# First cross-attention of a decoder: keys and queries projected without padding, heads moved to their 32-row blocks by DMA

## The reference

```
def _L0_xattn_ref(query, key_value, Wq, bq, Wk, bk, Wv, bv, Wo, bo):
    scale = D ** (-0.5)                                   # D = 16, H = 16
    q = (query @ Wq + bq).reshape(B, Nq, H, D).transpose(0, 2, 1, 3)
    k = (key_value @ Wk + bk).reshape(B, Nkv, H, D).transpose(0, 2, 1, 3)
    v = (key_value @ Wv + bv).reshape(B, Nkv, H, D).transpose(0, 2, 1, 3)
    attn = jnp.einsum('bhqd,bhkd->bhqk', q, k) * scale
    attn = jax.nn.softmax(jnp.clip(attn, -CLAMP, CLAMP), axis=-1)
    x = jnp.einsum('bhqk,bhkd->bqhd', attn, v).reshape(B, Nq, Cq)
    return x @ Wo + bo
...
x = _layernorm(x + _L0_attn_ref(x, ...))
x = _layernorm(x + _L0_xattn_ref(x, ctx_768, ...))
x = _layernorm(x + _L0_ffn_ref(x, ...))
```

## Time and profile before

| | |
|---|---|
| median of 3 runs | 1327.05 us (1320.21 to 1327.78) |
| the profiled execution | 1310.7 us, its span 1309.0 us |
| PE busy | 1163.7 us, 89% of the span |
| DVE, ACT, POOL busy | 56%, 43%, 7% |
| PE's granted clock, mean | 0.952 of full |
| A0 and X0 | 0 to about 465 us of the span |
| X0's steady part | about 220 to 440 us |

### The profile page before, as it was taken

How to read it: one execution, slowest core, us unless ns; L and a number is a source line. 1 busy time by engine, 2 the same in 40 slices (tenths; PEclk the granted TensorE clock), 3 DMA queues, 4 the chain that set the end, 5 groups by cost and what they waited for, 6 DMA issues and landing times.

```text
span 1309.0 us, 20311 instructions
## 1 busy us (share of the span) xinstructions
PE 1163.7 (89%) x7602; PEld 737.1 (56%) x7602; DVE 734.4 (56%) x1083; ACT 560.2 (43%) x1078; POOL 86.6 (7%) x126
## 2 busy tenths in 40 slices
PE   4998988898998864897799999999999999998886
PEld 2454443232322233786477777767777777776545
DVE  3447567888889747344265645654445554654322
ACT  1444424555555632120266654555334553453230
POOL 0112301000000002000000000000000000000120
PEclk8899778999999977999899999999999999999989
DMA  6011002000000020000533222323533333210000
GB/s 178 11 50 26 1 1 57 1 1 1 1 1 1 1 81 1 1 1 1 139 74 74 66 66 46 80 57 89 116 92 82 81 82 81 47 36 1 1 17 16
DMA packets 46819, 57.44 MB, mean 44 GB/s; under 512 B 12539, under 2 KB 25350, under 8 KB 46726
## 3 DMA queue, kind: packets, MB, share of 16 engines
q1 hardware_dynamic: 42966, 52.48, 16.4%
q10 hardware_dynamic: 3760, 3.67, 0.9%
HBM read 15.23 MB, written 3.15 MB: 14 GB/s over the span
## 4 chain that ended last, share of the span: by engine, by line
PE 77%; DVE 10%; issue 6%; ACT 3%; POOL 1%; DMA 1%; SPq 1%; POOLq 0%; ACTq 0%; DVEq 0%
PE p_unit L1529 20%; PE p_ring L1529 11%; PE p_ring L1630 9%; PE p_out L1653 8%; PE p_ring L1549 8%; PE p_ring L1596 7%; PE p_out L1619 6%; PE p_ring L1574 2%; PE p_unit L1715 2%; PE p_unit L1673 1%; DVE probT_b L1342 1%; PE p_ring L1588 1%; DVE stats L1245 1%; ACT prob_a L1130 1%; POOL m_z L1059 1%
## 5 line engine op out<-in xcount | busy, mean ns | idle before, releaser
L1148 ACT ACTIVATE probT_b<-p_ring 128x512 f32<-128x512 f32 x144 | 84.5, 598 | 260.0 <-PE p_ring L1630 259.6
L1312 DVE TENSOR_REDUCE halves<-p_ring 128x2 f32<-128x1024 f32 x128 | 155.6, 1219 | 44.2 <-PE p_ring L1574 44.0
L1342 DVE COPY probT_b<-p_ring 128x512 f32<-128x512 f32 x112 | 77.4, 691 | 173.7 <-PE p_ring L1630 173.7
L1294 DVE TENSOR_REDUCE nmax<-p_ring 128x2 f32<-128x1024 f32 (+1 forms) x128 | 155.9, 1218 | 23.3 <-PE p_ring L1549 23.3
L1130 ACT ACTIVATE prob_a<-p_ring 128x1024 f32<-128x1024 f32 x128 | 130.5, 1023 | 89.5 <-PE p_ring L1596 89.2
L1116 ACT ACTIVATE prob_b<-p_ring,nmax 128x512 f32<-128x512 f32 (+1 forms) x192 | 158.7, 835 | 2.9 <-DVE nmax L1294 2.6
L1549 PE MATMUL p_ring<-stacks 128*128 128x512 f32 x512 | 150.8, 416 | 4.5 <-ACT prob_b L1116 4.5
L1630 PE MATMUL p_ring<-ident,prob_b 128*128 128x128 f32 x1024 | 134.6, 274 | 0.0
L1630 PEld LDWEIGHTS p_ring<-ident,prob_b 128*128 128x128 f32 x1024 | 115.8, 141 | 27.7 <-issue 25.8
L1596 PE MATMUL p_ring<-x_q,x_kq 32*128 32x512 f32 x512 | 117.8, 646 | 0.2
L1549 PEld LDWEIGHTS p_ring<-stacks 128*128 128x128 f32 x512 | 87.0, 190 | 17.1 <-ACT prob_b L1116 5.1
(11 more groups left out here) (199 smaller groups left out, 1610.4 us busy)
## 6 DMA issues: line engine op xcount, KB each, us to landing
stacks<-splitH_b SPq DMA_DIRECT2D x144, 128.0 KB, 2.3
stacks<-splitL_b SPq DMA_DIRECT2D x144, 128.0 KB, 2.4
a_st<-a_image SPq DMA_DIRECT2D x64, 32.0 KB, 1.8
ctx_raw<-in_ctx ACTq DMA_DIRECT2D x1, 1536.0 KB, 15.2
x<-in_x ACTq DMA_DIRECT2D x2, 512.0 KB, 5.5
k_words<-in_L_ffn_k SPq DMA_DIRECT2D x1, 1024.0 KB, 6.7
a_wq<-in_L_attn_Wq SPq DMA_DIRECT2D x1, 1024.0 KB, 6.0
a_wo<-in_L_attn_Wpost SPq DMA_DIRECT2D x1, 1024.0 KB, 8.6
```

The source lines that it names most:

```text
L1294: nc.vector.tensor_reduce(nmax[:, n % 4, 0:heads], src, AX.X, ALU.max, negate=True).then_inc(done["M"], 1)
L1312: nc.vector.tensor_reduce(to, src, AX.X, ALU.max, negate=True).then_inc(done["M1"], 1)
L1342: keep_turned(dve, key, lambda o, i: nc.vector.tensor_copy(o, i)).then_inc(done["VD"], 1)
```

## The change

Keys and queries of X0 are projected in slices of 128 true columns, eight heads at once, so one product serves two groups: 12 units in place of 24. ACT empties them into a new tile `x0_dense` (three parts of 512: two for keys, one for queries), which holds one pair of groups. A new kind of "DS" step on SP then moves each head's 16 rows to its 32-row block of `x0_kq`: 12 DMAs of 16 partitions a group, 96 in all, counted on one semaphore for each place (`x0_spread`). The padding and the row of ones, which the padded weights used to produce, are written once, by two memsets of `x0_kq` on DVE ahead of the stream. The query's factor moves from the weights into ACT's instruction, and the spread copies of the weights fall away.

POOL rounds a group's three parts only when its 12 DMAs have landed. ACT may overwrite `x0_dense` only when the DMAs of the pair's second group have landed (`heads_whole`); the ring place is waited for on SP and no longer on ACT. S1 of a group comes at least five steps after its DS step.

The context transposes (cT) now all stand ahead of the keys. The keys of groups 2 and 3 (pair 0, 1) are projected in A0 of batch 1, after the first query unit. The pairs (1, 0) and (1, 1) are projected at the ends of groups 0 and 2 of X0; the ends of groups 1, 3 and 4 have no projection any more. The S1, S2, PV and transposes of X0 keep their steps.

```diff
--- before.py
+++ after.py
...
@@ -164,7 +164,7 @@
...
-        return age("KF", "q", L, b, g) >= 2 and all(age("KF", "k", L, b, g, h) >= 2 for h in range(2))
+        return age("DS", L, b, g) >= 5
...
-            if u[0] in ("k", "q") and u[1] == "X0":
-                sched.add("KF", *u)
...
-    def x0_keys(b, g):
-        n = 4 * b + g - HELD
-        return [unit("k", "X0", b, g, h, after=used(8 + n) if n >= 0 else []) for h in range(2)]
-
-    def x0_queries(b, g):
-        n = 4 * b + g - HELD
-        return [unit("q", "X0", b, g, after=[turned_x("A0", b)] + (used(8 + n) if n >= 0 else []))]
+    def x0_heads(b, c):
+
+        G = 4 * b + 2 * c
+        out = [unit("k", "X0", b, c, s, after=[("DS", ("X0", (G - 1) // 4, (G - 1) % 4))] if G else []) for s in range(2)]
+        out.append(unit("q", "X0", b, c, after=[turned_x("A0", b)]))
+        for g in (2 * c, 2 * c + 1):
+            n = 4 * b + g - HELD
+            out.append(step("DS", "X0", b, g, after=[UA("q", "X0", b, c)] + (used(8 + n) if n >= 0 else [])))
+            out += [step("KF", b, g, part) for part in range(3)]
+        return out
...
-        [unit("cT", sg, c) for sg in range(2) for c in range(2)] + x0_keys(0, 0) + x0_keys(0, 1)
-        + [unit("cT", sg, c) for sg in range(2, 4) for c in range(2)] + x0_keys(0, 2)
-        + x0_keys(0, 3) + [u for g in range(4) for u in x0_keys(1, g)],
-        [q for b in range(B) for g in range(4) for q in x0_queries(b, g)],
+        [unit("cT", sg, c) for sg in range(4) for c in range(2)],
+        [it for b in range(B) for c in range(2) for it in x0_heads(b, c)],
...
-        x0_wq = sb("x0_wq", [128, 2, 512], into=first)
-        x0_wk1 = sb("x0_wk1", [128, 512], into=first)
+        x0_wq = sb("x0_wq", [128, 2, C], into=first)
+        x0_wk1 = sb("x0_wk1", [128, C], into=first)
+        x0_dense = sb("x0_dense", [128, 3, 512], into=first)
...
+
+            n = 4 * b + g
+            eng.wait_ge(x0_spread[n % HELD], 16 * 12 * (n // HELD + 1))
...
-            sp.dma_start(wq_in[:, :, :], rows("L0_xattn_Wq")).then_inc(x0_loaded, 16)
-            sp.dma_start(wk_in[:, 0, :], d["L0_xattn_Wk"][0:128, :]).then_inc(x0_loaded, 16)
-            sp.dma_start(wk_in[0:CC - 128, 1, :], d["L0_xattn_Wk"][128:CC, :]).then_inc(x0_loaded, 16)
-            sp.dma_start(wk_in[64:65, 1, :], d["L0_xattn_bk"].rearrange("(o n) -> o n", o=1)).then_inc(x0_loaded, 16)
+            sp.dma_start(x0_wq[:, :, :], rows("L0_xattn_Wq")).then_inc(x0_loaded, 16)
+            sp.dma_start(x0_wk0[:, :], d["L0_xattn_Wk"][0:128, :]).then_inc(x0_loaded, 16)
             sp.wait_ge(pads_cleared, 1)
+            sp.dma_start(x0_wk1[0:CC - 128, :], d["L0_xattn_Wk"][128:CC, :]).then_inc(x0_loaded, 16)
+            sp.dma_start(x0_wk1[64:65, :], d["L0_xattn_bk"].rearrange("(o n) -> o n", o=1)).then_inc(x0_loaded, 16)
             sp.dma_start(x0_wv0[:, 0:C], d["L0_xattn_Wv"][0:128, :]).then_inc(x0_loaded, 16)
             sp.dma_start(x0_wv1[0:CC - 128, 0:C], d["L0_xattn_Wv"][128:CC, :]).then_inc(x0_loaded, 16)
             sp.dma_start(x0_wv1[64:65, 0:C], d["L0_xattn_bv"].rearrange("(o n) -> o n", o=1)).then_inc(x0_loaded, 16)
-            bq = d["L0_xattn_bq"].rearrange("(g a p) -> a p g", a=4, p=16)
-            for a in range(4):
-                sp.dma_start(x0_bq[32 * a:32 * a + 16, :], bq[a], allow_slow_non_contiguous=True).then_inc(x0_loaded, 16)
+            sp.dma_start(x0_bq[:, :], d["L0_xattn_bq"].rearrange("(c p) -> p c", p=128),
+                         allow_slow_non_contiguous=True).then_inc(x0_loaded, 16)
...
+                if L == "X0":
+                    grp = 4 * b + p
+                    place, c = grp % HELD, p // 2
+                    sp.wait_ge(heads_cleared, 1)
+                    wait(sp, "UA", "k", "X0", b, c, 0)
+                    wait(sp, "UA", "k", "X0", b, c, 1)
+                    wait(sp, "UA", "q", "X0", b, c)
+                    if grp >= HELD:
+                        wait(sp, "S2", *prob_items(PAIRS[8 + grp - HELD])[-1])
+                    for part in range(3):
+                        for a in range(4):
+                            at = 64 * (p % 2) + 16 * a
+                            sp.dma_start(x0_kq[32 * a:32 * a + 16, place, part, :], x0_dense[at:at + 16, part, :])\
+                              .then_inc(x0_spread[place], 16)
+                    continue
...
-            pool.wait_ge(x0_scaled, 1)
...
-                    u = key
-                    _, L, b, g = u[:4]
-                    place, part = (4 * b + g) % HELD, u[4] if u[0] == "k" else 2
-                    wait(pool, "UA", *u)
+                    b, g, part = key
+                    place = (4 * b + g) % HELD
+                    heads_whole(pool, b, g)
...
-                        _, L, b, g = u[:4]
-                        place, part = (4 * b + g) % HELD, u[4] if u[0] == "k" else 2
-                        if 4 * b + g >= HELD:
-                            wait(act, "S2", *prob_items(PAIRS[8 + 4 * b + g - HELD])[-1])
+                        _, L, b, c = u[:4]
+                        if 4 * b + 2 * c:
+                            n = 4 * b + 2 * c - 1
+                            heads_whole(act, n // 4, n % 4)
                         if u[0] == "q":
-                            ins = nc.scalar.activation(x0_kq[:, place, part, :], p_unit[:, :], ACT.Identity,
-                                                       bias=x0_bq[:, g:g + 1])
+                            act.wait_ge(x0_scaled, 1)
+                            ins = nc.scalar.activation(x0_dense[:, 2, :], p_unit[:, :], ACT.Identity,
+                                                       bias=x0_bq[:, c:c + 1], scale=LAYERS["X0"]["D"] ** -0.5)
                         else:
-                            ins = nc.scalar.activation(x0_kq[:, place, part, :], p_unit[:, :], ACT.Copy)
+                            ins = nc.scalar.activation(x0_dense[:, u[4], :], p_unit[:, :], ACT.Copy)
...
-            for t in (x0_wv0, x0_wv1):
-                nc.vector.memset(t[:, :], 0.0)
-            nc.vector.memset(x0_bq[:, :], 0.0).then_inc(pads_cleared, 1)
+            nc.vector.memset(x0_wk1[:, :], 0.0)
+            nc.vector.memset(x0_wv1[:, :], 0.0).then_inc(pads_cleared, 1)
...
             nc.vector.memset(wide_max[:, :, :, :], 0.0)
-            nc.vector.memset(x0_wq[:, :, :], 0.0)
-            nc.vector.memset(x0_wk0[:, :], 0.0)
-            link(nc.vector.memset(x0_wk1[:, :], 0.0))
-            nc.vector.memset(x0_wk1[64:65, :].rearrange("p (h r) -> p h r", r=32)[:, :, 16], 1.0)
             nc.vector.memset(ctx_sum1[64:128, :], 512.0)
             nc.vector.memset(ctxT1[64:128, :], 1.0).then_inc(ctx_padded, 1)
+            nc.vector.memset(x0_kq[:, :, 0:2, :], 1.0)
+            nc.vector.memset(x0_kq[:, :, 2, :], 0.0).then_inc(heads_cleared, 1)
 
             for kind, key in sched.steps:
                 if kind == "XW":
-                    k = LAYERS["X0"]["D"] ** -0.5
                     dve.wait_ge(x0_loaded, 16 * X0_LOADS)
-                    for c in range(2):
-                        nc.vector.tensor_scalar(x0_wq[:, c, :].rearrange("p (h r) -> p h r", r=32)[:, :, 0:16],
-                                                wq_in[:, c, :].rearrange("p (h d) -> p h d", d=16), k, None, ALU.mult)
-                    nc.vector.tensor_copy(x0_wk0[:, :].rearrange("p (h r) -> p h r", r=32)[:, :, 0:16],
-                                          wk_in[:, 0, :].rearrange("p (h d) -> p h d", d=16))
-                    nc.vector.tensor_copy(x0_wk1[0:65, :].rearrange("p (h r) -> p h r", r=32)[:, :, 0:16],
-                                          wk_in[0:65, 1, :].rearrange("p (h d) -> p h d", d=16))
-                    nc.vector.tensor_scalar(x0_bq[:, :], x0_bq[:, :], k, None, ALU.mult).then_inc(x0_scaled, 1)
+                    nc.vector.tensor_scalar(x0_bq[:, :], x0_bq[:, :], LAYERS["X0"]["D"] ** -0.5, None, ALU.mult)\
+                      .then_inc(x0_scaled, 1)
...
-                        wait(pe, "KF", "q", L, b, g)
-                        wait(pe, "KF", "k", L, b, g, hf)
+                        wait(pe, "KF", b, g, hf)
+                        wait(pe, "KF", b, g, 2)
...
-                            pe.wait_ge(x0_scaled, 1)
+                            pe.wait_ge(x0_loaded, 16 * X0_LOADS)
```

16 lines of the change are left out of this document (7 added, 9 removed).

## The result

The changed kernel takes 1355.35 us (median of 6 runs, 1352.62 to 1363.47) against 1319.82 us (median of 6 runs, 1316.30 to 1327.78): a ratio of 1.028, 95% interval 1.024 to 1.032. The forecast was 1342.6 us with a range up to 1353. A second comparison, later, gave 1343.6 us (4 runs, 1332.76 to 1348.05) against 1318.29 us, a ratio of 1.015 (1.006 to 1.024), by the medians 1.019. In short: the projections of three groups in X0 came back as forecast; the stretches with new waits for DMAs cost 41.8 us, clock included, where 32.4 were forecast; and A0 of batch 0 has two levels, some 18 us apart, where the forecast had a single saving.

The account below looks back on a forecast made before the run. PE sets the pace where units run, DVE a floor. -13.35 + 8.2 + 15.2 + 2.4 - 5.9 + 9 = +15.6 us: 1326.3 on the profiled execution, 1342.6 on the median of 1327.05; range 1329 to 1353.

Parts of the forecast that it names:

- A0 of batch 0: Six key units stood here, two stay; four units fewer, less some 0.5 us each taken back: -5.9 us.
- -3.5: Forecast lateness at the 56th reduction, ahead of the first new wait: +2.4 us at the start, -5.9 for key units.
- the issue interval of 0.458 us: SP's time per new DMA in X0 and A0 of batch 1, taken from 24 gathers issued in 11.00 us.
- the 56 intervals of the sum: Issue intervals between DMAs in the forecast's waits in A0 and X0: 23 + 11 + 2 x 11, each 0.458 us.
- What is saved in X0: Groups 1, 3 and 4 of X0 lose their three projections each, at 4.45 us a group: -13.35 us.
- What is waited for in X0: Two groups that still project wait through ACT for 12 DMAs, PE 4.1 us late each: +8.2 us.
- What is waited for in A0: A0 of batch 1: ACT waits for 24 DMAs, then a shorter chain through POOL; whole place +15.2 us.
- just in time for PV: A0 of batch 1: POOL's six casts ahead of its affine_selects end a little after, in time for PV.
- slow issue: Rival: each DMA issue takes 0.597 us, adding +7.8 us in X0 and A0; +23.4 us, 1350; chance 0.13.
- Cheap issue: Rival: DMAs go out nearly at once, only A0's added unit is left; -14.9 us, 1312; chance 0.10.
- The start: The two x0_kq memsets on DVE, less those removed, delay a0_L and the scatter: +2.4 us.
- PE's clock behind the pauses: After three new pauses in A0 and X0, PE's slower clock costs 3 us each, +9; bounds 0 and 3.4 each.

Follow-up runs that it names:

- first trace of before: The unchanged kernel before, the first execution profiled, zero point of the lateness measure; 1310.7 us.
- before with late keys: Kernel before with the key units of groups 1 and 2 moved behind the first X0 query unit; 1323.85 us, ratio 0.999.
- With the memsets on POOL: Changed kernel with two dense tiles, four DMAs a group, later casts, x_kq memsets on POOL, pair (0, 0) and (0, 1) keys among context transposes; 1304.51 us, ratio 0.989.
- two tiles and late casts: Changed kernel with two dense tiles used in turn and POOL's casts placed later; 1303.8 us, ratio 0.989.

## Why the prediction was wrong

By the profiled executions, forecast 1326.3 and measured 1353.9, 27.6 us are missing. A0 of batch 0 has 18.3 of them (14.8 against -3.5), the waits in A0 of batch 1 5.1 (23.3 against 15.2 and 3 for the clock), the two waits in X0 4.3 (18.5 against 8.2 and 6 for the clock); the three groups are right to 0.2. These make 27.9.

So two steps failed. The larger is the term of -5.9 us for A0 of batch 0, which priced the clock there at nothing: this execution has 41 us of half clock in it. The smaller is the issue interval of 0.458 us, in whose place 0.625 was measured; over the 56 intervals of the sum that is 9.4 us, less 1.2 for four landings of 2.0 us in place of 2.3, and PE's idle time was 9.1 us over the forecast's. The first trace of before flatters part of the rest: against three of its four further traces the place in A0 of batch 1 costs 2.7 us less.

By the times, the change costs 35.5 us where 15.6 were forecast. That 1355.35 is only 12.8 us over 1342.6 is luck: the forecast stood on a median of three runs, which was 7 us too high.

- **What is saved in X0: right.** 13.35 us was forecast, and each of the three groups gives 4.4 us, 13.2 in all, in every kernel of the table that has the change (5.3 is this and the two waits; -13 is this alone). Pricing a unit by the step's period, 4.45 for three units of 1.98, was what made it right; by PE's busy time it would have been 17.8. Busy time by stretch in the changed kernel, a group without units, has PE and DVE where the second line of the earlier trace rows has them:

```profile
376.00:407.00 31.00, 26.55 (x170) 8.19 (x164) 29.78 (x38) 17.66 (x33) 2.03 (x3) 1.00 0.06 13
```

- **What is waited for in X0: mechanism right, size off.** The failed step is "24 gathers of 16 partitions were issued in 11.00 us, 0.458 us each": the new DMAs start 0.63 us apart ((282.00 - 275.13) / 11 = 0.625). PE's idle time was 5.72 us in both places against 4.1; each place cost 8.3 and 10.2 us with the clock.
- **What is waited for in A0: mechanism right, size off by the same step.** PE was idle 12.96 us against 8.9, and 6.10 us through POOL where the forecast, by the end of its chain, had 4.3. The remark that the six casts end "just in time for PV" hid that POOL's wait is enough by itself; it would have shown that a second dense tile alone saves nothing there.
- **The rival "slow issue" was the one that held.** It took 0.597 us from the DMAs of 64 partitions and gave +23.4 us; the changed kernel at full clock in A0 of batch 0 was 1332.8 us, 22.1 over the first trace of before. Its 1350 us lies near the measured 1355.35 by luck, since it too has -3.5 for A0 of batch 0. "Against it: 16 partitions, as in the gathers" chose the wrong likeness: those gathers read DRAM, and in one trace the two kinds have medians of 0.420 and 0.589 us at equal bytes and partitions. That the source makes the difference was not tested by itself.
- **Cheap issue: wrong.** The Trainium skill, "DMA: Bandwidth & Descriptors", Anatomy of one DMA, which stood beside it, is a section on DMAs issued from POOL, and these come from SP. Its some 2 us for one DMA agrees with the landing here, 2.0 us; what it says of emitting many descriptors did not carry over to many DMAs, of which twelve took 7.46 us to issue.
- **The start: right.** The first reduction is 2.2 us late for 2.4 forecast. Timeline of DVE, changed kernel:

```profile
16.61 2.62 DVE L1284 MEMSET x_kq<- 128x3072 f32 x1 [0.70 <-issue]
19.50 1.34 DVE L1285 MEMSET x_kq<- 128x1536 f32 x1 [0.27 <-issue]
20.75 0.63 DVE L1485 TENSOR_TENSOR a_L<-p_unit,a_H 128x512 fp32r<-128x512 f32 x1
```

  Eight reductions on, it is between 1.3 early and 0.6 late in the three traces, but key steps are gone by then too: before with late keys, the same stream without the memsets, is 2.4 early there, so 1.1 to 3.0 us of the term still stand. With the memsets on POOL the first reduction was 1.6 us early, and the time no better than with two tiles and late casts.
- **A0 of batch 0: wrong as a single number.** Where the clock holds, -3.5 forecast and -4.0 measured; where it doesn't, +14.0 and +14.8. The prediction looked for a clock price only behind new pauses. Its baseline was part of this: the trace of 1310.7 us is at full clock throughout that stretch, and the 16 us by which it is under the median came from three runs, 1327.05 us, where more runs put the median at 1318 to 1320. What makes the clock fall there stays open.
- **PE's clock behind the pauses: about right.** Busy time by stretch behind the first X0 pause and the second:

```profile
282.00:286.00 4.00, 1.28 (x2) 0.76 (x3) 0.00 (x0) 1.60 (x3) 1.73 (x3) 0.63 0.10 23
286.00:290.00 4.00, 4.00 (x9) 0.92 (x8) 0.00 (x0) 0.60 (x1) 0.00 (x0) 0.52 0.00 0
...
358.00:362.00 4.00, 2.70 (x3) 1.18 (x4) 0.00 (x0) 1.60 (x3) 1.73 (x3) 0.52 0.01 3
362.00:366.00 4.00, 4.00 (x9) 1.00 (x8) 0.82 (x1) 1.46 (x2) 0.00 (x0) 0.50 0.00 0
366.00:370.00 4.00, 4.00 (x14) 1.13 (x16) 1.21 (x3) 1.18 (x4) 0.00 (x0) 0.70 0.00 0
```

  The lateness less the idle time is 8.3 - 5.7 = 2.6 and 10.2 - 5.7 = 4.5 us, for 3 each; the second is over the upper bound of 3.4. With four DMAs a group the pause is 1.87 us, the clock stays at full, and the place costs 1.9 and 2.0 us:

```profile
269.38 1.98 PE L1533 MATMUL p_unit<-ctxT,x_wk 128*128 128x512 f32 x4 [1.87 <-ACT x_dense L1210]
```

## What to carry to other kernels

Price a run of DMAs in front of a wait by its issues, with an issue time from DMAs of the same source and destination, and count what stands behind each engine that waits for them: here 2 x 12 issues held ACT and POOL, each enough to hold PE, and only a second buffer together with later casts turned 2.8% lost into 1.1% won. Merge DMAs before they are moved about: 96 KB were issued in the time of 32. Issuing part of the DMAs from another engine was not tried. Where PE's clock drops in some executions and not in others, one trace of before is no baseline for a stretch; take several, one of them of a time near the median.
